# Four graph layers on one core: transformer blocks written out with norms by node tiles across the seams, graph convolution joined to them, and another order of VectorE's work in the one-hot sums

## The chip, the core and the metric

One Trainium2 chip, one of its cores. A core has TensorE (matrix products into PSUM), VectorE, ScalarE and GpSimd (elementwise work), SyncE (here only the start of DMAs) and 16 DMA engines. Each engine runs its own list of instructions in order and waits on semaphores for the others. The metric is the time of one execution on the device, in microseconds (us); the lower the better. In the profile TensorE's products are PE, its weight loads PEld, VectorE is DVE, ScalarE is ACT, GpSimd is POOL, SyncE is SP; a q behind a name means the engine's sequencer.

## What is computed

Four graph layers follow each other on 625 nodes with 512 features and 20,000 edges (src, dst), sorted by dst. Each gets h = relu(layernorm(x)) and adds its result to x:

```python
x = x + _L0(h)   # relu(mean of h[src] over the edges of dst @ W_l.T + b_l + h @ W_r.T)
x = x + _L1(h)   # four transformer blocks, below
x = x + _L2(h)   # graph convolution: sum of h[row]*norm over the edges, @ lin_w.T + lin_b
x = x + _L3(h)   # edge network with mish, sums by node, layernorm
...
for i in range(NUM_BLOCKS):                                   # 4
    y = _cond_layer_norm(x, cond, s1_w[i], s1_b[i], b1_w[i], b1_b[i])   # xn*(1+scale)+bias
    y = _sparse_attention(y, src, dst, wq[i], bq[i], wk[i], bk[i], wv[i], bv[i], wo[i], bo[i])
    x = x + y
    y = _cond_layer_norm(x, cond, s2_w[i], s2_b[i], b2_w[i], b2_b[i])
    y = jax.nn.relu(y @ m_w1[i] + m_b1[i]) @ m_w2[i] + m_b2[i]
    x = x + y
```

scale and bias come from a 16-wide vector per node (cond). Attention has 4 heads of 128 and runs over the edges; several equal edges count severally.

## The kernel before

The 625 nodes are padded to NP = 640, five node tiles of 128 rows (NT = 5); 512 features are four chunks (KF = 4). `build` runs four stages, each a block of its own with a barrier at its end: `front`, `transformer_layer`, `gcn_layer`, `edge_layer`.

**front** turns the edges into dense 640 x 640 matrices: how often an edge occurs, and its weight in two f16 parts. The edges go in 40 groups of 512. For a group VectorE compares the edges' targets with 64 node numbers (the to-comparison, L531) and the sources of three of its four tiles with all 640 (three from-comparisons, L535); ScalarE makes the fourth tile from |difference| (L334, L337); GpSimd multiplies the to-matrix by the weights (L314, 128x512 f16) as soon as the to-comparison is done; TensorE multiplies from and to (20 products of 192 columns into one of two PSUM places), and VectorE adds the result to `sums` (L556, PSUM and SBUF). `compare(u + 2, ...)` stands two groups ahead of the addition of group u. The loop is a hardware loop (`Fori`) with four groups per turn; two groups are compared ahead of it.

**transformer_layer** has a hardware loop over the four blocks. Every product with a weight matrix is made of f32r parts: high (rounded, by ScalarE, `high`) and low (the rest, by VectorE, `low`), and is three matmuls, hi*hi, hi*lo and lo*hi. A block on TensorE: norm(0) with v, then q and k (transposed, in parts of 384 and 256 nodes), attention in N = 20 steps of head and node tile (scores S, transposed probabilities T, and after each head's tiles the product o), wo by node tiles, norm(1), m1 (transposed), m2 by node tiles. Two PSUM banks `one` and three double banks `two` are handed out in a fixed order by `Plan`.

A norm, in the order of the engines: VectorE has the statistics of each tile (L1052) right behind the residual addition (L1050); after the fifth tile it aggregates all five (L1014), adds EPS (L1016); ScalarE takes the inverse root of all five by Ln and Exp (L178, L180); VectorE normalizes a tile (L1023) and scales it by TensorE's product of cond (L1029 after L840); TensorE turns it and adds the bias product (L832, L835); ScalarE takes the high part (L934) and VectorE the low part (L1036) out of PSUM. GpSimd adds the row bias to the residual r as soon as VectorE has normalized a tile (L791), and cuts the cond weights (L780). SyncE loads a weight matrix into one of two places when the matrix before in that place has been split.

**gcn_layer** loads the kept weight matrix (1600 KB) and lin_w, makes the norm on VectorE for all tiles, then eight sums of five products (`agg`) and five products with lin_w (`lin`). **edge_layer** is not changed.

## Time and profile before

| what | us |
|---|---|
| timed runs, median of 3 (lowest to highest) | 1864.12 (1862.62 to 1864.5) |
| the profiled execution, its own time | 1859.79 |
| its span, first to last instruction | 1858.1 |
| front (loop over the edge groups in it) | 0 to 212.4 (16.6 to 142.1) |
| transformer blocks | 212.4 to 966.4 |
| graph convolution | 966.4 to 1016.6 |
| edge network | 1016.6 to 1858.1 |
| busy: PE, DVE, ACT, POOL | 1640.7, 1258.9, 1028.6, 678.1 |

A row of the trace has the start of an instruction (or of several alike in a row), how long it or they took, the engine, the line, the operation, output and inputs by name with their sizes, and in brackets how long the engine had been idle before and what it had waited for. "issue" is idle time for which the profile shows no wait. The names C, tr_two and tr_one in the norm's rows are the normalized tile y, a `two` bank and a `one` bank.

### The profile page before, as it was taken

The page shows a single profiled execution, that of the slowest core. Times are in us where ns is not written, and L with a number is a line of the kernel's source. Part 1 is how long each engine was busy: PE and PEld are TensorE (multiplying, and loading weights), DVE is VectorE, ACT ScalarE, POOL GpSimd, SP SyncE. Part 2 cuts the span into 40 slices and gives each one's busy share as a digit, 9 for nine tenths or more (in the row PEclk, how much of TensorE's full clock was granted, in tenths as well). Part 3 has the DMA queues.
Part 4 walks back from the last instruction along what each step waited for, and adds up shares of the span by engine and source line. Part 5 has one row for each costly group of instructions (what it writes and reads, how often), then busy time and mean ns, then how long its engine had stood idle before and what let it go on. Part 6 is the DMA issues. An engine that isn't in the chain of part 4 may idle for free. (4 is left out here: it accounts for less than half of the span.)

```text
span 1858.1 us, 26597 instructions
## 1 busy us (share of the span) xinstructions
PE 1640.7 (88%) x8590; PEld 1278.8 (69%) x8590; DVE 1258.9 (68%) x1915; ACT 1028.6 (55%) x1292; POOL 678.1 (36%) x497
## 2 busy tenths in 40 slices
PE   4559699889988998899868879999999999999986
PEld 3555296679667966786654367777777777777863
DVE  8997646553646364536463358888888888888844
ACT  7643125232523262326131069999999999999822
POOL 2330100120012001200110277888888888888200
PEclk9999799989998999899889989999999999999988
DMA  2000421021102200220020676777777777778400
GB/s 94 0 0 1 147 60 46 1 69 58 45 1 70 80 23 6 70 74 23 6 86 30 207 161 144 143 140 149 145 141 147 145 141 148 146 139 186 91 29 29
DMA packets 109491, 158.94 MB, mean 86 GB/s; under 512 B 42459, under 2 KB 47579, under 8 KB 108803
## 3 DMA queue, kind: packets, MB, share of 16 engines
q0 software_dynamic: 74320, 89.02, 24.6%
q1 hardware_dynamic: 35090, 68.86, 11.7%
q8 instruction: 48, 0.79, 0.2%
q14 instruction: 33, 0.26, 0.0%
HBM read 145.73 MB, written 11.86 MB: 85 GB/s over the span
## 5 line engine op out<-in xcount | busy, mean ns | idle before, releaser
L1416 POOL DMA_INDIRECT edge_early<-dst_table,edge_index x160 | 311.3, 1946 | 63.9 <-issue 55.3
L194 PE MATMUL edge_z2p<-edge_w_hi,edge_h_hi 128*128 128x512 f32 x640 | 261.7, 409 | 0.4 <-issue 0.2
L791 POOL TENSOR_TENSOR tr_r<-tr_r,tr_row_b 128x512 f32<-128x512 f32 x40 | 54.8, 1393 | 565.2 <-DVE C L1023 565.2
L194 PE MATMUL edge_z2p<-edge_w_hi,edge_h_lo 128*128 128x512 f32 x640 | 253.6, 396 | 0.0
L194 PE MATMUL edge_z2p<-edge_w_lo,edge_h_hi 128*128 128x512 f32 x640 | 253.4, 396 | 0.0
L1385 POOL DMA_INDIRECT edge_early<-src_table,edge_index x160 | 175.1, 1094 | 96.5 <-issue 36.8
L194 PEld LDWEIGHTS edge_z2p<-edge_w_hi,edge_h_hi 128*128 128x128 f32 x640 | 120.5, 188 | 54.7 <-issue 29.1
L194 PEld LDWEIGHTS edge_z2p<-edge_w_hi,edge_h_lo 128*128 128x128 f32 x640 | 120.5, 188 | 29.2
L194 PEld LDWEIGHTS edge_z2p<-edge_w_lo,edge_h_hi 128*128 128x128 f32 x640 | 120.7, 189 | 25.3
L1684 DVE TENSOR_TENSOR edge_late<-edge_z2p,edge_b 128x1024 f32<-128x1024 f32 x80 | 97.9, 1224 | 51.3 <-PE edge_z2p L194 50.9
L194 PE MATMUL front_sum_ps<-front_to_onehot,front_from_onehot 128*128 128x192 f16 x800 | 74.7, 251 | 59.1 <-DVE front_sums L556 45.9
L959 ACT ACTIVATE tr_probs<-tr_scores,tr_nmax 128x640 f32<-128x640 f32 x80 | 66.2, 828 | 109.1 <-DVE tr_nmax L1080 106.2
L1080 DVE CUSTOM_DVE_ANT_0 tr_scores<-tr_two,logc 128x640 f32<-128x640 f32 x80 | 65.9, 824 | 85.7 <-PE tr_two L866 84.1
L194 PE MATMUL tr_one<-tr_yT_hi,tr_w_hi 128*128 128x256 f32 (+1 forms) x384 | 121.3, 316 | 2.6 <-DVE tr_kT L1068 2.6
L194 PE MATMUL tr_one<-tr_yT_lo,tr_w_hi 128*128 128x256 f32 (+1 forms) x384 | 119.9, 312 | 0.0
L194 PE MATMUL tr_one<-tr_yT_hi,tr_w_lo 128*128 128x256 f32 (+1 forms) x384 | 119.7, 312 | 0.0
L1701 DVE SCALAR_TENSOR_TENSOR edge_early<-edge_early,edge_z1p 128x1024 f32<-128x1024 f32 x80 | 97.3, 1217 | 31.7 <-ACT edge_early L1592 30.4
L194 PEld LDWEIGHTS front_sum_ps<-front_to_onehot,front_from_onehot 128*128 128x128 f16 x800 | 66.8, 100 | 67.1 <-issue 53.2
L1582 ACT ACTIVATE edge_early<-edge_z1p 128x1024 f32<-128x1024 f32 x80 | 80.5, 1006 | 50.3 <-PE edge_z1p L1471 50.3
L866 PE MATMUL tr_two<-tr_kT,tr_qT 128*128 128x320 f32 x320 | 100.9, 442 | 5.4 <-ACT tr_probsT L965 4.1
L1588 ACT ACTIVATE edge_early<-edge_early 128x1024 f32<-128x1024 f32 x80 | 84.4, 1055 | 36.7 <-DVE edge_early L1662 35.9
L1462 PE MATMUL edge_z1p<-ident,edge_early 128*128 128x128 f32 x640 | 84.8, 276 | 17.9 <-DMA edge_early<-dst_table,edge_index 13.2
(300 smaller groups left out, 4054.4 us busy)
## 6 DMA issues: line engine op xcount, KB each, us to landing
edge_attr<-in_attr_T SPq DMA_DIRECT2D x80, 128.0 KB
tr_w_raw<-in_m SPq DMA_DIRECT2D x8, 1024.0 KB, 5.3
tr_w_raw<-in_wv SPq DMA_DIRECT2D x5, 1024.0 KB, 5.3
tr_w_raw<-in_wq SPq DMA_DIRECT2D x5, 1024.0 KB, 5.4
agg<-edge_sum_rows POOLq DMA_DIRECT2D x37, 128.0 KB
tr_w_raw<-in_wk SPq DMA_DIRECT2D x4, 1024.0 KB, 7.4
tr_w_raw<-in_wo SPq DMA_DIRECT2D x4, 1024.0 KB, 5.3
tr_cw_raw<-in_cond_w SPq DMA_DIRECT2D x5, 768.0 KB, 5.6
```

Source lines behind the costliest of these rows:

```text
L194: mm = pe.matmul(out, a, b, start=(n == 0), stop=(n == last))
L791: pool.tensor_tensor(r[:, i, :], r[:, i, :], row_b[:, :], ALU.add).then_inc(bias_added, 1)
L866: mm = pe.matmul(bank[:, f, 0:HALF], qT[:, h, i * P:(i + 1) * P], kT[:, h, f * HALF:(f + 1) * HALF], start=True, stop=True)
L959: act.activation(probs[:, n % 3, :], scores[:, n % 2, :], ACT.Exp, bias=nmax[:, n:n + 1], scale=-1.0, accum_out=den[:, n:n + 1]).then_inc( ...
L1080: ins = dve.tensor_tensor_reduce(out=cols(scores[:, n % 2, :], HALF), in0=bank[:, :, 0:HALF], in1=cols(k.logc[:, i, :], HALF), scale=-1.0, ...
L1385: pool.indirect_dma_start(out=from_rows[a][:, j, :], out_offset=None, in_=k.src_table, in_offset=bass.IndirectOffsetOnAxis(ap=index[a // 2 ...
L1416: pool.indirect_dma_start(out=from_rows[ring][:, j, :], out_offset=None, in_=k.dst_table, in_offset=bass.IndirectOffsetOnAxis(ap=index[rin ...
L1462: mm = pe.matmul(z1[:, c, j * P:(j + 1) * P], from_rows[ring][:, j, c * P:(c + 1) * P], k.ident[:, :], is_transpose=True, start=(c % 2 == ...
L1582: act.activation(m1[one], ps_z1[one][:, :], ACT.Exp).then_inc(S["e1_ready"], 1)
L1588: act.activation(m1[one], m1[one], ACT.Square).then_inc(S["inner1_ready"], 1)
L1684: dve.tensor_tensor(cols(z2[two], D), cols(ps_z2[:, :], D), b2[:, None, :].to_broadcast([P, PT, D]), ALU.add).then_inc(S["z2_ready"], 1)
L1701: dve.scalar_tensor_tensor(m1[one], m1[one], 0.5, ps_z1[one][:, :], ALU.subtract, ALU.mult).then_inc(S["h1_ready"], 1)
```

## The change

Three things are changed.

1. In the one-hot loop `compare` is cut in two. VectorE's order in a group is now: to-comparison of group u + 2, addition of group u, three from-comparisons of group u + 2.
2. `transformer_layer` and `gcn_layer` become one function, `transformer_and_gcn`, and the loop over the blocks is a Python loop: the four blocks are written out in each engine's program, with constants where registers stood. A norm goes tile by tile and is laced into the products before it: behind the residual of a tile follow its statistics, their aggregate and the negated mean on VectorE, then on ScalarE Ln, Exp, mean times root and the normalized tile itself (an activation with bias and scale, in place of VectorE's L1023). TensorE has the scale product of tile i and the turning of tile i - 2 between two tiles of wo, or of m2 for the next block's norm; the last tile is turned within m1, or between the first two tiles of v. The scale product lies in the second half of a `two` bank, the turned tile in its first. For wo's first two tiles the products over the first three heads are made early, at steps 19 and 21 of attention. low("m1") and low("wv") go in four pieces, between steps or tiles. GpSimd adds the row bias after all five tiles are normalized; in the last block it also adds r to x.
3. The convolution lies behind the last block without a barrier. Its matrix is loaded when the last head's product has been read, its norm goes by tiles as above (with the factor `dis` on ScalarE), and its first two sums run over tiles 0 to 3 before tile 4 is added.

```diff
@@ front
-                        compare(u + 2, (a + 2) % RING, start_of(u + 2))
+                        compare_to(u + 2, (a + 2) % RING, start_of(u + 2))
                         start = start_of(u)
...
                             "p (i n w) -> p i n w", i=NT, n=4)[:, :, 0:3, :], ALU.add).then_inc(added, 1)
+                        compare_from(u + 2, (a + 2) % RING)
@@ TensorE
-                with pe.Fori(0, BLOCKS) as b:
-                    pe.wait_ge(block_done, b + 1)
-                    norm(0, b)
+                def step(b, s, i):
+                    scale(b, s, i)
+                    if i >= 2:
+                        feature_major(b, s, i - 2)
...
+                for b in range(BLOCKS):
+                    if b == 0:
+                        for i in range(NT):
+                            step(b, 0, i)
+                    feature_major(b, 0, 3)
+                    value(b, 0)
+                    feature_major(b, 0, 4)
+                    for i in range(1, NT):
+                        value(b, i)
...
+                        if n == N - 1:
+                            plan.open(pe, ("early", b))
+                            plan.need(pe, ("o", b, HEADS - 2, 1))
+                            wait_weights("wo", b)
+                            early(0)
+                        if n == N + 1:
+                            early(1)
...
                     for i in range(NT):
-                        by_node("wo", i, "wo", rows, b)
-                    norm(1, b)
+                        if i < 2:
+                            if i == 0:
+                                plan.need(pe, ("o", b, HEADS - 1, 0))
+                            plan.made(three(plan.at[("wo", b, i)].bank[:, :],
+                                            node_pairs(of_tile(rows, i), "wo", [HEADS - 1]), start=False))
+                        else:
+                            if i == 2:
+                                plan.need(pe, ("o", b, HEADS - 1, 1))
+                            by_node("wo", i, of_tile(rows, i), "wo", b)
+                        step(b, 1, i)
+                    feature_major(b, 1, 3)
...
                         for m in range(KF):
                             by_feature("m1", m, f, "m1", b)
+                            if (f, m) == (0, 1):
+                                feature_major(b, 1, 4)
...
-                        by_node("m2", i, "m2", (hid_hi, hid_lo, yT_hi, yT_lo), b)
+                        by_node("m2", i, hidden_tile(i), "m2", b)
+                        if b < LAST:
+                            step(b + 1, 0, i)
...
+                pe.wait_ge(loaded["gcn_W"], 16)
+                for m in range(2):
+                    plan.open(pe, ("agg", m, 0))
+                    neighbours(m, 0, range(NT - 1))
+                for m in range(2):
+                    plan.made(neighbours(m, 0, [NT - 1]))
@@ ScalarE
+                def inverse(i, factor=None):
+                    act.wait_ge(var_ready, inverse.n + 2)
+                    inverse.n += 1
+                    own(act.activation(k.rstd[:, i:i + 1], inverse.mv[:, i, 1:2], ACT.Ln, bias=eps[:, 0:1]))
+                    own.wait()
+                    own(act.activation(k.rstd[:, i:i + 1], k.rstd[:, i:i + 1], ACT.Exp, scale=-0.5))
+                    own.wait()
...
+                    own(act.activation(shift[:, i:i + 1], neg_mean[:, i:i + 1], ACT.Copy, scale=k.rstd[:, i:i + 1]))
+                    own.wait()
...
+                def step(b, s, i):
+                    if i >= 2:
+                        high_part(b, s, i - 2)
+                    inverse(i)
+                    act.activation(y[:, i, 0:D], r[:, i, :], ACT.Identity, bias=shift[:, i:i + 1],
+                                   scale=k.rstd[:, i:i + 1]).then_inc(y_ready, 1)
...
                     for i in range(NT):
+                        step(b, 1, i)
+                    high_part(b, 1, 3)
+                    plan.take(act, ("wo", b, NT - 1))
+                    high("m2", b)
+                    high_part(b, 1, 4)
@@ VectorE
+                def step(b, s, i):
+                    moments(i, r, st, mv)
+                    if i >= 2:
+                        low_part(b, s, i - 2)
+                    if i >= 1:
+                        scaled(b, s, i - 1)
...
+                    for i in range(NT):
+                        residual("wo", b, 0, i)
+                        step(b, 1, i)
+                    scaled(b, 1, NT - 1)
+                    low_part(b, 1, 3)
+                    low("m2", b)
+                    low_part(b, 1, 4)
...
+                    if b < LAST:
+                        for i in range(NT):
+                            residual("m2", b, 1, i)
+                            step(b + 1, 0, i)
+                            if i < PIECES:
+                                low_piece("wv", b + 1, i)
@@ GpSimd
-                            pool.wait_ge(read1, b * (2 * NT) + (s * NT + i + 1))
+                        pool.wait_ge(y_ready, of_norm(b, s, NT - 1))
+                        for i in range(NT):
                             pool.tensor_tensor(r[:, i, :], r[:, i, :], row_b[:, :], ALU.add).then_inc(bias_added, 1)
+                        if b < LAST:
+                            pool.wait_ge(bias_added, of_norm(b, s, NT - 1))
+                            cut(b + 1, s)
```

How the lists of two engines read before and now. First VectorE in the one-hot loop, one group; ISA and REGISTER_ALU rows are its sequencer's. Before:

```order
L525 TENSOR_LOAD starts
L525 ISA x2
L531 ISA
L531 TENSOR_TENSOR front_to_onehot<-front_iota,front_dst 128x4x64
L535 ISA
L535 TENSOR_SCALAR front_from_onehot<-front_iota,front_src_f 128x640
...
L552 REGISTER_ALU
L556 ISA
L556 TENSOR_TENSOR front_sums<-front_sums,front_sum_ps 128x15x64
```

and now:

```order
L556 TENSOR_TENSOR front_to_onehot<-front_iota,front_dst 128x4x64
L550 TENSOR_LOAD starts
L550 ISA x2
L582 REGISTER_ALU
L586 ISA
L586 TENSOR_TENSOR front_sums<-front_sums,front_sum_ps 128x15x64
L564 ISA
L564 TENSOR_SCALAR front_from_onehot<-front_iota,front_src_f 128x640
```

The addition to front_sums has moved from behind the three from-comparisons to between them and the to-comparison.

VectorE again, at the seam from wo to m1, from the fourth wo tile before:

```order
L1050 TENSOR_TENSOR tr_r<-tr_r,tr_one 128x512
L110 REGISTER_ALU
L1052 BN_STATS tr_st<-tr_r 128x6
L76 REGISTER_ALU
L1014 BN_AGGR tr_mv<-tr_st 128x2 x5
L76 REGISTER_ALU
L1016 TENSOR_SCALAR rstd<-tr_mv 128x5
L1017 REGISTER_ALU
L1023 TENSOR_SCALAR C<-tr_r,tr_mv,rstd 128x512 x2
```

and now, third and fourth tile:

```order
L1222 TENSOR_TENSOR tr_r<-tr_r,tr_one 128x512
L1193 BN_STATS tr_st<-tr_r 128x6
L1195 BN_AGGR tr_mv<-tr_st 128x2
L1197 TENSOR_SCALAR tr_neg_mean<-tr_mv 128x1
L1209 TENSOR_TENSOR tr_yT_lo<-tr_two,tr_yT_hi 128x4x128
L1202 SCALAR_TENSOR_TENSOR C<-tr_two,C 128x512
L1222 TENSOR_TENSOR tr_r<-tr_r,tr_one 128x512
```

Each tile now has its own aggregate, and the low part of the tile two before and the scaling of the tile before stand ahead of the next residual.

TensorE at the same seam, before: the last products of wo, then the norm.

```order
L194 MATMUL tr_one<-tr_w_hi,tr_yT_lo 128x512
L825 REGISTER_ALU
L110 REGISTER_ALU
L840 MATMUL tr_one<-tr_cw,condT 128x512
L110 REGISTER_ALU
L840 MATMUL tr_one<-tr_cw,condT 128x512
L110 REGISTER_ALU x2
L832 MATMUL tr_two<-ident,C 128x128 x4
L835 MATMUL tr_two<-condT,tr_cw 128x128 x4
```

Now, at the end of wo's third tile and the start of its fourth:

```order
L883 MATMUL tr_one<-tr_w_lo,tr_yT_hi 128x512
L883 MATMUL tr_one<-tr_w_hi,tr_yT_lo 128x512
L911 MATMUL tr_two<-tr_cw,condT 128x512
L919 MATMUL tr_two<-ident,C 128x128 x4
L922 MATMUL tr_two<-condT,tr_cw 128x128 x4
L883 MATMUL tr_one<-tr_w_hi,tr_yT_hi 128x512
```

The scale product and the turning of an earlier tile stand between two tiles of wo. TensorE's program has 2934 such rows, before 1452.

## Rows read from the trace of the kernel before

**Rows 1.** Busy us (count) by stretch: PE, PEld, DVE, ACT, POOL; clock; DMA.

```profile
16.64:142.09 125.45, 74.74 (x800) 66.76 (x800) 125.42 (x209) 69.00 (x107) 47.59 (x40) 1.00 0.00 2
391.84:575.00 183.16, 164.27 (x816) 133.34 (x815) 95.47 (x177) 64.78 (x114) 18.51 (x12) 0.93 0.14 44
```

**Rows 2.** The same view, one group of the loop, and the last but one.

```profile
103.61:106.68 3.07, 1.81 (x20) 1.61 (x20) 3.07 (x6) 1.54 (x3) 1.19 (x1) 1.00 0.00 0
137.39:139.68 2.29, 1.81 (x20) 1.61 (x20) 2.29 (x6) 0.00 (x0) 0.00 (x0) 1.00 0.03 7
```

**Rows 3.** Timeline (start, us, engine, line, operation): the same two groups.

```profile
103.61 0.41 DVE L531 TENSOR_TENSOR front_to_onehot<-front_iota,front_dst 128x256 f16 x1
...
104.53 1.16 DVE L535 TENSOR_SCALAR front_from_onehot<-front_iota,front_src_f 128x640 f16<-128x640 f16 x1
...
104.32 1.19 POOL L314 TENSOR_TENSOR front_to_onehot<-front_to_onehot,front_wb 128x512 f16<-128x512 f16 x1 [1.88 <-DVE front_to_onehot L531]
105.61 1.14 DVE L556 TENSOR_TENSOR front_sums<-front_sums,front_sum_ps 128x960 f32 x1
...
137.73 0.97 DVE L535 TENSOR_SCALAR front_from_onehot<-front_iota,front_src_f 128x640 f16<-128x640 f16 x3
```

**Rows 4.** Busy by stretch as in rows 1: seams, attention, the last m2.

```profile
362.00:376.27 14.27, 10.57 (x47) 9.33 (x45) 11.40 (x22) 2.81 (x6) 6.85 (x5) 0.63 0.08 20
...
406.60:420.43 13.83, 7.67 (x29) 6.51 (x30) 9.41 (x19) 1.90 (x5) 6.85 (x5) 0.62 0.14 52
...
465.00:511.00 46.00, 42.02 (x200) 29.21 (x199) 28.33 (x70) 26.38 (x51) 0.00 (x0) 1.00 0.13 45
...
943.98:958.70 14.72, 14.16 (x62) 11.00 (x60) 9.94 (x11) 4.53 (x5) 4.79 (x2) 1.00 0.00 0
958.70:972.90 14.20, 0.02 (x1) 0.00 (x0) 12.32 (x28) 1.70 (x3) 0.00 (x0) 0.65 0.38 135
```

**Rows 5.** Timeline of PE: the last head, the norm, in m1.

```profile
341.28 5.64 PE L194 MATMUL tr_one<-C,tr_v 128*128 128x320 f32 x20 [0.87 <-ACT C L965]
...
366.59 1.12 PE L832 MATMUL tr_two<-ident,C 128*128 128x128 f32 x4 [3.14 <-DVE C L1029]
...
379.25 0.36 PE L194 MATMUL tr_one<-tr_yT_hi,tr_w_hi 128*128 128x384 f32 x1
```

**Rows 6.** Waits of PE (us in total, times, longest): loop's turn; all blocks.

```profile
PE tr_one L840 <- issue: 4.2, 1, 4.2
...
PE tr_two L874 <- DVE tr_probs L1090: 17.7, 40, 1.3
```

**Rows 7.** Timeline: the convolution's first product, and the last sum's copy.

```profile
973.40 0.87 PE L194 MATMUL gcn_p<-gcn_W,gcn_h 128*128 128x320 f32 x1 [14.68 <-DMA gcn_W<-W_kept]
...
996.81 0.44 ACT L1148 ACTIVATE gcn_aggT<-gcn_p 128x320 f32<-128x320 f32 x1 [2.25 <-PE gcn_p L194]
```

**Rows 8.** Timeline of the norm between wo and m1.

```profile
362.20 0.69 DVE L1050 TENSOR_TENSOR tr_r<-tr_r,tr_one 128x512 f32<-128x512 f32 x1 [1.33 <-PE tr_one L194]
362.92 0.69 DVE L1052 BATCH_NORM_STATS2 tr_st<-tr_r 128x6 f32<-128x512 f32 x1
...
364.45 0.21 ACT L178 ACTIVATE rstd<-rstd 128x5 f32<-128x5 f32 x1 [17.05 <-DVE rstd L1016]
...
365.55 1.50 POOL L791 TENSOR_TENSOR tr_r<-tr_r,tr_row_b 128x512 f32<-128x512 f32 x1 [129.94 <-DVE C L1023]
365.85 0.68 DVE L1029 SCALAR_TENSOR_TENSOR C<-tr_one,C 128x512 f32<-128x512 f32 x1
```

**Rows 9.** Timeline: an activation with bias and scale in front.

```profile
52.12 0.80 ACT L365 ACTIVATE front_h<-x,front_shift,rstd 128x512 f32<-128x512 f32 x1
```

**Rows 10.** Timeline of PE: a tile turned among v, q's start in blocks 2 and 1.

```profile
424.70 0.60 PE L832 MATMUL tr_two<-ident,C 128*128 128x128 f32 x4
...
437.62 0.34 PE L194 MATMUL tr_one<-tr_yT_hi,tr_w_hi 128*128 128x384 f32 x1
...
253.18 0.34 PE L194 MATMUL tr_one<-tr_yT_hi,tr_w_hi 128*128 128x384 f32 x1
```

674 lines of the change are left out of this document (359 added, 315 removed).

## Prediction

> **What bounds the kernel now.** I read the sums by stretch first [rows 1]. Up to 142 us VectorE is busy all the time (the one-hot loop), from 212 to 1017 us TensorE is the fullest engine but has holes, and the edge stage, 841 us, is not touched by the change. So two things are to be found: what fills VectorE in the loop, and what makes TensorE's holes at the seams of a transformer block.
>
> In the loop one group of edges takes 3.07 us on VectorE, the last groups only 2.29 us [rows 2]. The difference is one instruction: of three equal comparisons the third lasts 1.16 us and ends at 105.69, 0.18 us after GpSimd's multiplication ended at 105.51 [rows 3]. The last two groups have no multiplication left. So the multiplication holds the comparison. TensorE (1.81 of 3.07 us) and ScalarE (1.54) wait for VectorE, not it for them [rows 2].
>
> In a block, read the clock and TensorE's busy time in the seams [rows 4]. Between the end of the wo products and the start of m1 14.3 us pass, between m2 and v 13.8 us, at 0.62 and 0.63 of the full clock; the clock sinks to its lower level (1.2 GHz) after the idle 3.14 us [rows 5] and comes back only inside m1. What TensorE waits for is the norm: all five tiles' statistics, then one root, then the tiles. Between two blocks comes 4.2 us in which TensorE waits for nothing shown ("issue"), at the turn of the loop [rows 6]. Before the graph convolution a barrier, a load and a norm leave TensorE idle for 14.68 us [rows 7].
>
> **1. The loop's order.** Nothing is added or removed. A group's order was to-comparison, three from-comparisons, addition; it becomes to-comparison, addition, three from-comparisons. From [rows 3], counted from the start of the to-comparison: the next VectorE instruction starts at 0.33, GpSimd starts at 0.71 (104.32 less 103.61) and ends at 1.90. The addition (1.07 from start to start) now lies under it, and the first from-comparison starts at 1.40. It is held to 1.90 and ends 0.18 later, 2.08, in place of 1.40 + 0.37 = 1.77 (0.37 is a comparison unheld: 0.97 for three, overlapped). So 0.31 us of holding stays, the group takes 2.29 + 0.31 = 2.60, and 0.47 us fall away in each of the 38 groups with a multiplication: **18 us**. Bounds: no holding left, 38 x 0.78 = 30; nothing gained, 0. Next late would be TensorE: its group starts after the comparisons, takes 1.81 and is wanted 0.33 us after the start of the group after next: 1.1 us of slack. ScalarE has 1.0.
> This rests on the addition (one operand in PSUM) not being held itself. The row for it: the scaling at 365.85, also with one operand in PSUM, takes 0.68 us beside a GpSimd addition that runs from 365.55 to 367.05 [rows 8]. Were it otherwise, GpSimd would start at 1.47, end at 2.66, the comparison at 2.84, and the group would take 3.36, 11 us more in all.
> The Trainium skill, SBUF — State Buffer, section "SBUF: two separate sides", says that VectorE and GpSimd take a shared port in turn, whole instruction by whole instruction, and that VectorE needs it in its two-port modes or with two SBUF inputs. By that rule the addition is free, as forecast (18 us); with the port taken by every VectorE instruction it would be the 11 us more.
>
> **2. The wo-m1 seam, four times.** The norm now runs tile by tile between the products. Per tile, with spacings from [rows 8]: VectorE 0.72 (residual) + 0.72 (statistics) + 0.20 + 0.17 (two small ones, by ScalarE's 0.21) = 1.81, then 0.62 each for scaling and low part, 3.05 in all. ScalarE: four small ones of 0.24 (L178 is 0.21) = 0.96, a new 128x512 activation with bias and scale, 0.80 [rows 9], and the high part 0.60: 2.36. TensorE: 2.75 for twelve products (m2: five times as many end 14.7 us after 943.98, 0.5 of it a wait and 0.4 the last one's length [rows 4]), 0.25 scale, 0.85 for turning (424.70 to 425.55) [rows 10]: 3.85. No engine is full, but tile i's chain (1.81, 1.76, 0.7, 0.85, 0.6, 0.62) is 6.3 us long and VectorE keeps strict order. Going down the three lists from the end of the last head's product: wo tiles 2, 3, 4 start at 1.9, 6.3 and 10.1, the turning of tile 2 ends at 14.0, that of tile 3 waits for VectorE until 16.2 (a hole of 2.2), m1 starts at 17.1. Tile 4 is turned inside m1 (0.85); ScalarE, in order, reads the first m1 bank only after it, and the two banks of the ring make m1 wait another 1.8. m2 starts at 33.8. Before it took 341.28 + 5.64 to 391.84 = 44.9 [rows 1, 5].
> Against that, 18 products of wo now run early, in attention, two pieces of 2.06 us. The first needs the low part of head 2, which VectorE makes after the probabilities of step 18, some 2.1 us after TensorE is free, and both stand ahead of what the last head needs: its product starts 3.7 us later (4.1 of work and 2.1 of waiting, less the idle time that was there: 1.3 and 0.3 for probabilities [rows 6], 0.9 before the product [rows 5]). So 44.9 - 33.8 - 3.7 = 7.4 a block, **30 us**. GpSimd's bias additions now start after the fifth tile and fall beside low("m2"), which is wanted only 14 us later; that cover hides them. Bounds: 3 to 11 a block.
>
> **3. The m2-v seam, three times.** The same chain between m2's five tiles, with four pieces of low("wv") on VectorE (0.66 each, an estimate by size: 128x512, like the residual's 0.69), and without the loop's turn. Down the lists: m2 tiles at 0, 3.0, 6.0, 9.9, 13.7, v at 20.6, q at 35.2. Before: 391.84 to 437.62 = 45.8 [rows 1, 10]. **10.6 each, 32 us**; 4.2 of it is the turn. GpSimd stands in this order behind a cut that waits for ScalarE's, so its bias additions fall beside low("wq"), which one of them can hold for its 1.5 us [rows 8]: q has 1.3 to spare, cost 0.2. Bounds: 6 to 14.
>
> **4. The graph convolution joined.** Its matrix and weights are loaded during the last seam, the norm goes by tiles, and GpSimd has added x and r before m2 is done. The first two sums run over tiles 0 to 3 (8 x 0.54 = 4.3 us), longer than tile 4's chain of 1.81 + 1.2 + 0.8 = 3.8. Before: m2's start 943.98 to the last sum's end 996.8 = 52.8 [rows 4, 7]. Now 13.8 for m2, 0.2, and 8 x 2.70 = 21.6: 35.6. **17 us**; bounds 12 and 19.
>
> **5. Small terms.** low("m1") in four pieces: TensorE waited 17.7 us in all for probabilities [rows 6]; I take a quarter of it as due to the whole one on VectorE and gone with the pieces, **4 us**, bounds 0 and 8. In the first block there was no turn of a loop, and ScalarE, free only after its two cuts and high("wv"), now makes the tiles one at a time, with low("wv") between them on VectorE: v starts at 239.7, q at 256.8, before 253.18 [rows 10]: **-4 us**; bounds -7 and 0.
>
> Sum: 18 + 30 + 32 + 17 + 4 - 4 = **97 us**. The profiled execution took 1859.8, which gives 1763; the median of the three timed runs is 4.3 higher, 1864.1, and the forecast is made there: **1767 us**.
>
> **The rivals.**
> A, the clock: at each wo-m1 seam a hole of 2.2 us stays, and idle 3.14 us were followed by 12.7 us at 1.2 GHz (366.6 to 379.3) [rows 5]. If the holes of 2.2 do the same, m1 runs at half clock for as long and loses 6.3 us a block: 25 us, 1792. For it: nothing in the trace shows what 2.2 us do. Against: attention has a hole at nearly every step, up to 1.3 us, and its stretch stands at 1.00 [rows 4]. The Trainium skill, TensorE: Matmul & The Clock Gate, section "A second HAM failure mode: psum-queue depth-cycling", says that small idle times between groups of products make the clock swing; by it A holds and more (attention too), and the attention row speaks against it.
> B, the loop gains nothing: the comparison behind the addition is held as long as before, because GpSimd starts later than I count. 1785; with the addition itself held, 1796. Against it are the two rows named in 1.
> C, slower than before: written out, the blocks are no loop any more, and TensorE's program is 2934 rows in place of 1452, each run once. If code arrives late, as at the loop's turn (4.2 us), each such halt costs 4.2 us; from 23 halts, six a block, the whole gain is gone, and at eight a block it is 134 us, 1901. For: the halts at the turn exist. Against: the front and the first and last 16 steps of the edge stage are written out too, and their rows show no such halt.
> D, the change doesn't do what it says: order inside VectorE makes the tile chains serial, a seam saves only the loop's turn and part of the clock: 3 us a seam in place of 7.4 and 10.6, 1767 + 40 = 1807.
>
> **How the numbers follow.** Forecast 0.66, with terms that move together about 1750 to 1784; A 0.15; B 0.09; D 0.07; C 0.03. Two in ten may be left out: the range is 1745 to 1796. Upwards it takes in A and B, downwards the loop free of holding (up to 12 us more) and the seams' upper bounds in part. About 0.2% (4 us) is what a measurement can tell from no change. All cases but C lie beyond it below: faster 0.96, same 0.01, slower 0.03.
>
> **What would show it.** The loop's group at 2.6 us, the first comparison (not the third) long. No "issue" of 3 to 4 us between blocks. From m2 to m2 of the next block about 183.2 - 7.4 - 10.6 - 1 = 164 us [rows 1]. TensorE's clock in the seams at 1.00 (A: lower). TensorE's wait before the first sum of the convolution under 1 us. It is wrong if comparisons are held elsewhere, if the early wo pieces delay the last head by much more than 3.7, or if TensorE shows many new waits for "issue".

## The result

Over four runs of each the kernel after takes 1769.95 us (median; 1763.32 to 1773.72) and the kernel before 1864.31 us: a ratio of 0.9488, 95% interval 0.9457 to 0.952. The forecast was 1767, the range 1745 to 1796. The profiled execution of after took 1770.9 us, its span is 1769.2 us; that is 88.9 us less than the span of before.

The page of after, its line of busy times. VectorE's busy time falls by 52 us, 24 of it in the loop, where comparisons were held; ScalarE's rises by 65, above all because it now makes the norm's tiles.

```profile
PE 1615.3 (91%) x8590; PEld 1259.4 (71%) x8590; DVE 1206.8 (68%) x1912; ACT 1093.3 (62%) x1476; POOL 684.2 (39%) x500
```

The sums by stretch of after (columns as in [rows 1]): two lines from the one-hot loop, one group each; four wo-m1 seams, from the start of the last head's product to the start of m2; three m2-v seams, from the start of m2 to the start of q; and the graph convolution, from the start of m2 to the end of the last sum.

```profile
95.21:97.66 2.45, 1.82 (x20) 1.60 (x20) 2.45 (x7) 1.58 (x3) 1.04 (x1) 1.00 0.00 0
97.66:100.11 2.45, 1.82 (x20) 1.60 (x20) 2.45 (x7) 1.54 (x3) 1.04 (x1) 1.00 0.00 0
...
322.69:365.18 42.49, 38.37 (x205) 33.96 (x203) 22.49 (x40) 20.22 (x42) 8.32 (x5) 0.92 0.10 32
494.59:535.52 40.93, 36.80 (x205) 32.38 (x204) 23.11 (x40) 20.23 (x42) 8.35 (x5) 0.96 0.10 33
664.51:703.87 39.36, 35.24 (x204) 30.81 (x203) 23.10 (x40) 20.23 (x42) 8.35 (x5) 1.00 0.10 34
831.23:873.68 42.45, 38.34 (x204) 33.95 (x203) 24.55 (x40) 20.22 (x42) 15.46 (x10) 0.92 0.11 39
365.18:402.21 37.03, 34.93 (x168) 29.12 (x166) 23.69 (x41) 16.69 (x33) 7.30 (x4) 0.95 0.11 26
535.52:572.55 37.03, 34.92 (x167) 29.00 (x166) 23.61 (x41) 16.69 (x33) 7.29 (x4) 0.95 0.10 26
703.87:739.31 35.44, 33.33 (x167) 27.77 (x166) 23.71 (x41) 16.69 (x33) 7.29 (x4) 1.00 0.09 31
...
873.68:909.11 35.43, 35.43 (x143) 26.50 (x142) 12.27 (x27) 13.41 (x34) 0.00 (x0) 1.00 0.00 0
```

The loop's group takes 2.45 us, before 3.07 [rows 2]. The convolution takes 35.43 us, before 52.8. The seams are the part to look at: the same work takes 42.5, 40.9, 39.4 and 42.5 us, and the granted clock is 0.92, 0.96, 1.00 and 0.92; 37.0, 37.0 and 35.4 us at 0.95, 0.95 and 1.00. At full clock a wo-m1 seam takes 39.4 us and an m2-v seam 35.4 us, and the others are longer by 1.6 us or twice that; 1.6 us is what one fall to the lower clock costs here. Over the seven seams it is 3.1 + 1.6 + 0 + 3.1 + 1.6 + 1.6 + 0 = 11.0 us.

The timeline of TensorE in the first block of after shows the holes (in brackets the idle time before the row): ahead of the first early piece of wo, ahead of the turning of the fourth tile, and inside m1.

```profile
317.36 0.47 PE L883 MATMUL tr_two<-tr_w_hi,tr_yT_hi 128*128 128x512 f32 x1 [2.10 <-ACT C L1145]
...
344.42 1.12 PE L919 MATMUL tr_two<-ident,C 128*128 128x128 f32 x4 [2.11 <-DVE C L1202]
...
353.70 0.44 PE L883 MATMUL tr_one<-tr_yT_hi,tr_w_hi 128*128 128x384 f32 x1 [1.63 <-ACT tr_qT L1165]
```

By stretch, with the times of both profiled executions:

| Stretch | before | after | forecast | measured |
|---|---|---|---|---|
| up to q of block 1 (loop, first norm) | 253.2 | 231.6 | 18 - 4 = 14 | 21.6 |
| q to m2, four blocks | 555.4 | 532.6 | 30 + 4 = 34 | 22.9 |
| m2 to q of the next block, three times | 135.4 | 109.5 | 32 | 25.9 |
| last m2 and convolution sums | 52.8 | 35.4 | 17 | 17.4 |
| behind them | 861.3 | 860.1 | 0 | 1.2 |
| sum | 1858.1 | 1769.2 | 97 | 88.9 |

From m2 to m2 of the next block 170.3, 168.4 and 169.8 us pass, where the prediction named 164 as a sign.

### The profile page after: what moved, and what is told of

The parts are those of the page before. It is cut to its first block and busy times, and to the rows that moved or that the text cites. A ratio compares the mean times of both kernels' runs of the same rounds, so it can differ in the third digit from the quotient of the medians.

```text
span 1769.2 us, 25359 instructions
## 1 busy us (share of the span) xinstructions
PE 1615.3 (91%) x8590; PEld 1259.4 (71%) x8590; DVE 1206.8 (68%) x1912; ACT 1093.3 (62%) x1476; POOL 684.2 (39%) x500
## 5 line engine op out<-in xcount | busy, mean ns | idle before, releaser
L867 POOL TENSOR_TENSOR tr_r<-tr_r,tr_row_b 128x512 f32<-128x512 f32 x40 | 64.7, 1650 | 289.4 <-ACT C L1099 289.1
L856 POOL TENSOR_TENSOR tr_cw<-tr_cw_raw,tr_cw 32x1024 fp32r<-32x1024 f32 x8 | 19.4, 2425 | 374.4 <-ACT tr_cw L1063 374.3
```

## The experiments

Each was timed against the kernel before on one chip, in four to ten executions; e2_small_mult has one. The median of before moved between 1858 and 1865 us from one group of runs to the next, so ratios are compared. The theory: three effects carry the change (the port held in the loop; a chain by tiles in place of a barrier at each seam; the barrier before the convolution), and what is missing at the seams is the clock, which falls behind holes of about 2 us. The rivals: the sizes of single pieces (the early products of wo, the split of m1's matrix) were wrong, or the blocks written out cost something of their own.

### The loop's order alone (e1_loop_alone)

Edit on the kernel before:

```
-                        compare(u + 2, (a + 2) % RING, start_of(u + 2))
+                        compare_to(u + 2, (a + 2) % RING, start_of(u + 2))
...
                         dve.tensor_tensor(into, into, ps[a % 2][:, 0:NT * 4 * WIN].rearrange(
                             "p (i n w) -> p i n w", i=NT, n=4)[:, :, 0:3, :], ALU.add).then_inc(added, 1)
+                        compare_from(u + 2, (a + 2) % RING)
```

> The kernel before with one edit, the order inside the one-hot loop (to-comparison, addition, three from-comparisons). Theory: the loop's gain is independent of everything later, so the group takes 2.44 us as in the trace of after, 38 x 0.63 = 24 us go, about 1840 us, ratio 0.987. Rival (the prediction's own size): GpSimd's multiplication keeps its 1.19 us, group 2.60, 18 us, 1846, ratio 0.990. Second rival: part of the early start of the blocks came from something else than the loop, then the loop alone gives less than 18.

Measured: 1838.12 us against 1864.93, ratio 0.9881 (0.9851 to 0.9912). In its trace a group takes 2.44 us. So the loop gives 16 to 28 us by itself, which leaves room for 18 as well as 24; the group decides, by it 38 x 0.63 = 24. The first theory holds. Why 2.45 and not 2.60 shows in the timeline of after:

```profile
95.21 0.41 DVE L556 TENSOR_TENSOR front_to_onehot<-front_iota,front_dst 128x256 f16 x1
95.55 1.14 DVE L586 TENSOR_TENSOR front_sums<-front_sums,front_sum_ps 128x960 f32 x1
95.92 1.04 POOL L339 TENSOR_TENSOR front_to_onehot<-front_to_onehot,front_wb 128x512 f16<-128x512 f16 x1 [1.41 <-DVE front_to_onehot L556]
96.61 0.53 DVE L564 TENSOR_SCALAR front_from_onehot<-front_iota,front_src_f 128x640 f16<-128x640 f16 x1
```

GpSimd's multiplication starts 0.71 us after the to-comparison, as forecast, and ends at 96.96. The first from-comparison starts at 96.61, lasts 0.53 us in place of 0.37 and ends 0.18 us after the multiplication. Everything is as the prediction put it but the length of the multiplication: 1.04 us, not 1.19 [rows 3]. Before, it ran beside comparisons; now it runs beside an addition from PSUM. In after itself both lengths stand: the multiplications of the first two groups, which still have comparisons beside them, take 1.13 and 1.18 us, all later ones 1.04. So comparisons lengthen it, and the addition doesn't. That is 0.15 us a group, 38 times: the missing 5.7 us.

### A smaller multiplication, old order (e2_small_mult)

Edit on the kernel before (one of four tiles is multiplied; the other three are set to zero once, so their weighted sums are left out):

```
-  pool.tensor_tensor(to_onehot[a][:, :, 1:3, :], to_onehot[a][:, :, 0:1, :].to_broadcast(shape),
-                     weights[:, :, :, None].to_broadcast(shape), ALU.mult).then_inc(weighted, 1)
+  small = [P, 1, 2, WIN]
+  pool.tensor_tensor(to_onehot[a][:, 0:1, 1:3, :], to_onehot[a][:, 0:1, 0:1, :].to_broadcast(small),
+                     weights[:, 0:1, :, None].to_broadcast(small), ALU.mult).then_inc(weighted, 1)
```

> The kernel before, old order of the loop, but GpSimd multiplies only one of the group's four tiles (the sums of the other three are left out, so the output is not the reference's). Theory (the multiplication holds the third comparison until its own end): with a multiplication that ends before the third comparison starts, the three comparisons take 0.97 us together, the group 2.29 to 2.35 us in place of 3.07, about 28 us in all. Rival (the third comparison is slow because of its place before an addition that reads PSUM, or because of ScalarE's two activations): group stays at 3.0 us or above.

Measured, one execution: 1833.87 us. The timeline, one group:

```profile
103.47 1.11 DVE L539 TENSOR_SCALAR front_from_onehot<-front_iota,front_src_f 128x640 f16<-128x640 f16 x3
103.84 0.56 POOL L318 TENSOR_TENSOR front_to_onehot<-front_to_onehot,front_wb 128x128 f16<-128x128 f16 x1 [1.88 <-DVE front_to_onehot L535]
```

The group takes 2.43 us (103.13 to 105.56). The multiplication ends at 104.40, and the third comparison ends 0.18 us later, at 104.58; the three take 1.11 us, where 0.97 is free of holding. So the group is not at the 2.29 to 2.35 us that were expected: the short multiplication, too, ends after the third comparison has begun, and holds it for what is left. By the group it is 24 us, by the single time 31. The order is the old one, ScalarE does what it did: only the multiplication is shorter. So it holds the comparison, as the prediction had it; the rivals (place, ScalarE) fall. The Trainium skill, SBUF — State Buffer, section "SBUF: two separate sides", says that VectorE and GpSimd take the shared port whole instructions at a time, VectorE only in its two-port modes or with two SBUF inputs. These traces agree: 1.16 us beside 0.37 for the comparison, and 1.14 us for the addition with one operand in PSUM, before and after, alone or beside the multiplication.

### The blocks written out, nothing else (e3_written_out)

Edit on the kernel before, on all five engines:

```
-                with pe.Fori(0, BLOCKS) as b:
+                for b in range(BLOCKS):
```

> The kernel before with the four blocks written out on all five engines in place of a loop; nothing else is changed. Theory: what goes is VectorE's 3.0 us of waiting for nothing shown at each of three turns, on the path there: 9 us (the prediction took 4.2 a turn from TensorE's wait, 12.6), 1852 to 1855, ratio 0.993 to 0.995. Rival C: code that is run once arrives late: new waits of 3 to 4 us for nothing shown inside the blocks, no gain or a loss. Third: the turn is hidden by the norm that follows, ratio 1.000.

Measured: 1851.34 us against 1864.93, ratio 0.994 (0.9923 to 0.9958). VectorE's timeline at the first turn, of before and then of this kernel:

```profile
411.05 0.45 DVE L1014 BATCH_NORM_AGGREGATE tr_mv<-tr_st 128x2 f32<-128x6 f32 x5 [3.01 <-issue]
```

```profile
410.14 0.45 DVE L1014 BATCH_NORM_AGGREGATE tr_mv<-tr_st 128x2 f32<-128x6 f32 x5
```

VectorE's wait for nothing shown is 3.01, 2.57 and 2.48 us at the three turns, 8.1 together, and is gone in all three. The three m2-v seams take 126.8 us in place of 135.4: 8.6. Seam by seam it is 4.9, 1.1 and 2.5 us, for the lower clock lasts a different time in each; only the sum fits the waits. The prediction had taken TensorE's wait of 4.2 us, its longest (all three have 10.2); VectorE's stood on the path, since the norm begins there. No new wait for "issue" appears on TensorE inside the blocks: rival C falls.

### No early pieces of wo (e6_no_early)

Edit on the kernel after: the first two tiles of wo are computed whole behind the last head.

```
-                        if n == N - 1:
-                            plan.open(pe, ("early", b))
-                            plan.need(pe, ("o", b, HEADS - 2, 1))
-                            wait_weights("wo", b)
-                            early(0)
-                        if n == N + 1:
-                            early(1)
```

> The kernel after without the early pieces of wo: the first two node tiles of wo are computed whole after the last head. Theory by the prediction's numbers: the last head starts 3.7 us sooner in each block, the seam has 4.1 us more of products: 0.4 a block slower, so 1.6 us, ratio to before 0.950 against 0.949. Rival: the early pieces delay the last head by less than they save or the wait of 2.1 us ahead of the first one is not made up for: 0 to 3 us a block either way.

Measured: 1782.22 us, ratio 0.9566 (0.9535 to 0.9597). After is at 0.9488 and, in the second measurement below, at 0.952: the pieces are worth 9 to 14 us, and not the 1.6 that were expected. In the two profiled executions it is 13.2 us. From the end of k to the last head's product the time falls by 2.5, 3.0, 3.0 and 4.1 us (3.7 were taken), 12.7 in all; the 4.1 has a fall of the clock in after, so without it the delay is 2.5 to 3.0. From there to m2 it rises by 24.4: four times the 4.1 us of products, and the head's product itself runs slower, 8.3 us in all:

```profile
321.70:329.50 7.80, 7.80 (x21) 5.28 (x22) 0.49 (x1) 0.44 (x1) 0.00 (x0) 0.72 0.00 0
493.40:500.70 7.30, 7.29 (x21) 5.01 (x22) 0.49 (x1) 0.44 (x1) 0.00 (x0) 0.77 0.00 0
667.40:674.70 7.30, 7.30 (x21) 5.01 (x22) 0.49 (x1) 0.44 (x1) 0.00 (x0) 0.77 0.00 0
840.10:848.20 8.10, 8.05 (x21) 5.44 (x22) 0.49 (x1) 0.44 (x2) 0.00 (x0) 0.70 0.03 10
```

In after the head takes 5.54 us in all four blocks, here 7.3 to 8.1 at clock 0.70 to 0.77. The early pieces fill the end of attention, where TensorE otherwise waits 1.35, 0.78 and 0.79 us in a row for the last steps, and keep the clock. In the kernel before it is the same: its last heads take 5.6, 7.3, 5.7 and 7.2 us. Of the 13.2 us the blocks hold 24.4 - 12.7 = 11.7; another 2 stand ahead of q of the first block, where the edit changes nothing.

### After again (after_again)

> The kernel after, unchanged, as the measure for the three others. Theory (what is left of the seams' loss is the clock, which falls in some seams and not in others): the seams' times differ between this execution and the one shown (wo-m1 seam from the last head's start to m2 39.4, 40.9 or 42.5 us; m2-v seam 35.4 or 37.0), each time with the granted clock; at clock 1.00 they are 39.4 and 35.4. Rival: the same seams are slow in every execution, with a cause of their own. Ratio 0.946 to 0.952.

Measured: 1768.67 us (1763.09 to 1780.33), ratio 0.952 (0.947 to 0.957). Its seams:

```profile
494.40:533.90 39.50, 35.37 (x205) 30.99 (x204) 23.16 (x40) 20.25 (x42) 8.35 (x5) 1.00 0.10 34
828.50:870.90 42.40, 38.27 (x205) 33.86 (x204) 23.98 (x40) 20.24 (x42) 15.43 (x10) 0.92 0.11 39
365.00:402.00 37.00, 34.89 (x167) 28.98 (x166) 23.73 (x41) 16.71 (x33) 7.26 (x4) 0.95 0.11 27
533.90:569.40 35.50, 33.39 (x168) 27.77 (x167) 23.56 (x41) 16.71 (x33) 7.33 (x4) 1.00 0.10 27
```

Again 39.4 and 35.4 us at clock 1.00 and the same steps above it, but in other blocks: the second block's seams took 40.9 and 37.0 us in the first execution and take 39.5 and 35.5 here. The work is the same; what differs is whether the clock falls. The holes behind which it may fall are there in every block. The other runs fit: over the eight executions of after the shortest (1763.1 and 1763.3 us) have the highest mean clock, 0.977, and the longest (1780.3) the lowest, 0.968.

### The hole filled (e4_fill8)

Edit on the kernel after:

```
+                    if i == 3:
+                        for _ in range(8):
+                            pe.matmul(bank[:, :], k.condT[:, i * P:(i + 1) * P], cw[:, 2 * s, :], start=True, stop=True)
                     plan.need(pe, ("scale", b, s, i))
```

> The kernel after, with eight more products of the scale kind (their result is overwritten) ahead of the turning of the fourth tile in every norm, where TensorE waits 2.1 us. No work is saved. Theory (the hole of 2.1 us is what makes the clock fall): the granted clock behind it stays at 1.00 and the seams go to 39.4 and 35.4 us, up to 11 us less, 5 us at least as the holes of 1.6 and 1.5 behind ScalarE stay: ratio 0.943 to 0.946. Rival (the clock falls by chance, or through the number of products before, not the hole): the same ratio as after, 0.949, or slower by the extra products.

Measured: 1765.41 us, ratio 0.9491 (0.9461 to 0.9522). The expected time was missed: at least 5 us less were named, and the ratio is the rival's. The time alone decides nothing. The stretches behind the hole do, first of after and then of this kernel (the same place, the first block, some 2 us later in this execution), then this kernel's seams:

```profile
342.00:344.00 2.00, 0.30 (x3) 0.16 (x2) 1.90 (x6) 1.33 (x4) 0.00 (x0) 1.00 0.00 0
344.00:346.00 2.00, 1.58 (x8) 1.59 (x9) 1.05 (x2) 0.87 (x2) 0.93 (x1) 0.57 0.04 8
346.00:348.00 2.00, 2.00 (x9) 2.00 (x9) 0.69 (x1) 1.69 (x2) 2.00 (x3) 0.58 0.00 0
348.00:350.00 2.00, 2.00 (x13) 2.00 (x12) 1.18 (x1) 0.72 (x1) 2.00 (x2) 1.00 0.00 0
```

```profile
344.00:346.00 2.00, 2.00 (x12) 1.56 (x10) 1.90 (x6) 1.29 (x4) 0.00 (x0) 1.00 0.00 0
346.00:348.00 2.00, 1.78 (x14) 1.54 (x13) 1.09 (x2) 1.37 (x3) 0.88 (x1) 1.00 0.00 0
348.00:350.00 2.00, 2.00 (x13) 2.00 (x12) 0.69 (x1) 1.96 (x2) 2.00 (x3) 1.00 0.00 0
524.00:528.00 4.00, 4.00 (x16) 4.00 (x15) 1.41 (x3) 1.05 (x2) 0.00 (x0) 0.59 0.68 121
...
324.70:364.10 39.40, 37.17 (x213) 32.17 (x212) 23.13 (x40) 20.26 (x42) 8.34 (x5) 1.00 0.10 34
493.20:534.20 41.00, 38.77 (x213) 33.81 (x213) 23.12 (x40) 20.25 (x42) 8.34 (x5) 0.96 0.12 32
663.10:702.50 39.40, 37.18 (x212) 32.22 (x211) 23.13 (x40) 20.25 (x42) 8.35 (x5) 1.00 0.11 34
829.80:869.30 39.50, 37.27 (x212) 32.30 (x212) 25.32 (x40) 20.25 (x42) 16.05 (x10) 1.00 0.12 43
364.10:399.50 35.40, 35.19 (x175) 29.10 (x174) 23.70 (x41) 16.72 (x33) 7.27 (x4) 1.00 0.11 28
534.20:569.60 35.40, 35.19 (x175) 29.07 (x174) 23.60 (x41) 16.72 (x33) 7.28 (x4) 1.00 0.11 28
702.50:738.00 35.50, 35.28 (x176) 29.16 (x175) 23.67 (x41) 16.72 (x33) 7.30 (x4) 1.00 0.09 30
```

Behind the hole of 2.11 us after stands at 0.57 and 0.58; with the hole filled, at 1.00. Six of seven seams are at 1.00, where the two executions of after have two and four of seven. The one at 0.96 falls inside m1 (0.59 from 524 to 528 us), behind ScalarE's hole of 1.6 us, which was not filled. Is it more than chance? Behind this hole, where it is not filled, the clock fell at 4, 2, 3, 2 and 6 of seven places in the traces of after, after_again, e10, e9 and e6, at 17 of 35 in all; filled, at none of seven. So work without use, put into the hole, keeps the clock up behind it; this rests on one execution with seven places. The seams take 265.6 us together, where those of after take 274.7 and 270.1. The gain in the median, 3 to 5 us, is within the scatter: two falls behind the hole of 2.10 us at the end of attention stay (486.3 and 824.2 us), and q of the third block waits 2.38 us here, 1.23 in after.

### Another order at the seams (e5_order)

Edit on the kernel after, TensorE's part (the other engines follow; ScalarE makes m2's high part in four pieces between the first tiles of m1, and wk's between two of q):

```
-                    feature_major(b, 0, 3)
                     value(b, 0)
+                    feature_major(b, 0, 3)
+                    value(b, 1)
                     feature_major(b, 0, 4)
...
-                    feature_major(b, 1, 3)
...
-                            if (f, m) == (0, 1):
-                                feature_major(b, 1, 4)
+                            if f == 0 and m < 2:
+                                feature_major(b, 1, 3 + m)
```

> The kernel after with another order on the same work: the first product group of v stands ahead of the turning of the fourth tile, the first of m1 too; ScalarE makes the high part of m2's matrix in pieces between the first four tiles of m1 and that of wk after two of q. Theory: TensorE's holes go from 2.11 + 1.63 to about 1.4 us in the wo-m1 seam (2.3 x 4), from 2.1 + 1.4 to nearly none in the m2-v seam (3.5 x 3) and 2 us in the first block, and about 8 us come from the clock: 30 us less than after, about 1740, ratio 0.933. Rival: the pieces make ScalarE or VectorE late inside m1 (1.8 us of ScalarE for 2.1 of TensorE), m2 starts later, and half of it is lost: 0.941.

Measured: 1752.25 us, ratio 0.9432 (0.94 to 0.9465): the gain of the rival, but not by its mechanism. The wo-m1 seams take 37.0 to 38.7 us and the m2-v seams 33.2. What was lost lies in three places. At full clock an m2-v seam gains 2.2 us, and 3.5 were named. Three of the four wo-m1 seams still have a fall of the clock (0.59 from 504.7 to 508.5 us), behind a new wait of 1.56 us at the start of m1. And in q of the second and third block TensorE waits 2.06 and 3.43 us for ScalarE, with the clock at 0.68 from 565 to 570 us, around the longer one.

### The first early piece later (e7_order_early)

```
-                        if n == N - 1:
+                        if n == N:
                             plan.open(pe, ("early", b))
```

> As e5_order, and the first early piece of wo stands behind the transposes of step 18 and no longer ahead of them. Theory: the transposes (0.7 us) go into the wait of 2.10 us ahead of the early piece, and the last head starts 0.4 to 0.7 us sooner in each block: 2 to 3 us less than e5_order, ratio 0.932. Rival: the transposes start late themselves, and the wait only moves: no change.

Measured: 1743.66 us, ratio 0.9369 (0.934 to 0.9399), 0.0063 less than e5_order: 8.6 us, where 2 to 3 were expected. From the end of k to the last head 61.1 to 61.6 us pass in place of 61.9 to 63.3, and three of the four wo-m1 seams take 37.0 us, where one did. The moved transposes are 0.5 us a block of this, 2.2 in all, as expected; the rest goes with the clock, whose mean over a run is 0.975 to 0.980 here and 0.968 to 0.973 in e5_order. The hole in q is still there. ScalarE's and SyncE's timeline show its cause:

```profile
391.92 0.44 SPq L799 DMA_DIRECT2D tr_w_raw<-in_wk  x1
...
399.75 1.91 ACT L1072 ACTIVATE tr_w_hi<-tr_w_raw 128x2048 fp32r<-128x2048 f32 x1 [3.06 <-DMA tr_w_raw<-in_wk]
```

ScalarE waits for the load of wk, which SyncE issued at 391.92 us. Its buffer was free some 17 us sooner (the next kernel shows it); ahead of it in SyncE's queue stood the load of the next conditioning weights, which waited for GpSimd's cut (387.05 to 391.52).

### The load first (e8_load_first)

Edit on the kernel just above (e7_order_early); besides, ScalarE makes wk's high part at its old place:

```
-                    if b < LAST:
-                        sp.wait_ge(cw_ready, b * 2 + 2)
-                        load_cw(b + 1)
                     sp.wait_ge(w_split, of_weight("wv", b) + PIECES)
                     load("wk", b)
+                    if b < LAST:
+                        sp.wait_ge(cw_ready, b * 2 + 2)
+                        load_cw(b + 1)
```

> As e7_order_early, but ScalarE makes wk's high part at its old place (behind the last tile of v), and SyncE issues the load of wk ahead of that of the next conditioning weights, whose wait (GpSimd's cut of this block's, which stands behind ScalarE's work on wq) came first. Theory: the hole of 3.3 us (ScalarE waits for wk's load, TensorE for ScalarE) inside q in the second and third block, new in e5 and e7, was the load issued 9 us after its buffer was free; it goes, with the low clock behind it, and from q to the last head all blocks take about 90 us in place of 94 and 96: 10 us less than e7_order_early, about 1734, ratio 0.932. Rival: wk's load now takes bandwidth from wq's, q starts later by as much: same as e7, 0.937.

Measured: 1735.79 us (1733.85 to 1736.64), ratio 0.9319 (0.9298 to 0.9341): the time that was expected. The load is issued at 374.68 us, and all seven seams stand at full clock (four of them here):

```profile
374.68 0.37 SPq L799 DMA_DIRECT2D tr_w_raw<-in_wk  x1
...
321.10:358.10 37.00, 35.06 (x204) 30.78 (x204) 22.73 (x43) 20.37 (x45) 7.43 (x5) 1.00 0.06 18
801.60:838.50 36.90, 34.96 (x204) 30.73 (x203) 25.58 (x41) 20.38 (x45) 14.60 (x10) 1.00 0.13 45
358.10:391.30 33.20, 33.20 (x167) 27.74 (x167) 22.60 (x41) 16.70 (x33) 4.51 (x2) 1.00 0.14 53
678.60:711.80 33.20, 33.20 (x167) 27.71 (x166) 22.57 (x41) 16.70 (x33) 4.55 (x2) 1.00 0.16 54
```

From q to q of the next block it is 160.3, 160.3 and 160.2 us, and the five runs lie within 2.8 us, where those of after spread over 10 and 17; their mean clock is 0.978 to 0.980. This kernel is faster than both: 34 us below after. The sum: 2.4 x 4 and 2.2 x 3 us in the seams at full clock, 2.7 of the hole in q, 12.3 of the clock (11.0 in the seams, 1.3 in the fourth block's attention), 0.6 x 4 at the end of attention: 33.6.

### Two single pieces (e9_m1_whole, e10_load_only)

The split of m1's matrix whole, as before, in the kernel after:

```
-                        if n == 4:
+                        if n == 2:
                             plan.take(act, ("k", b, KF - 1, 1))
...
-                        if 4 <= n < 4 + PIECES:
-                            act.activation(w_hi[0][:, n - 4, :], w_raw[0][:, n - 4, :], ACT.Copy).then_inc(w_high, 1)
+                            high("m1", b)
...
+                        if n == 3:
+                            low("m1", b)
...
-                        if 5 <= n < 5 + PIECES:
-                            low_piece("m1", b, n - 5)
```

> The kernel after, with the high and low part of m1's matrix made whole at steps 2 and 3 of attention, as in the kernel before, in place of four pieces at steps 4 to 8. Theory by the prediction: the pieces take a quarter of TensorE's waits for probabilities away, 4 us in all; without them 4 us slower, ratio 0.951. Rival: the whole one falls where nothing waits for long, 0 to 1 us; or it makes one long wait at which the clock falls, then 5 us or more.

Measured: 1782.36 us, ratio 0.9574 (0.9546 to 0.9603), against 0.9488 and 0.952 of after: 10 to 16 us slower. The waits of TensorE for probabilities, in total, times and the longest, of after and then of this kernel:

```profile
PE tr_two L974 <- DVE tr_probs L1290: 10.0, 32, 0.8
```

```profile
PE tr_two L974 <- DVE tr_probs L1290: 16.3, 40, 1.2
```

These are 6.3 us, and 3.9 us are new waits for the transposed probabilities. From the end of k to the first head's product 18.5 us pass in place of 16.4, in each block. So the pieces are worth 8 us, twice the 4 that were taken. The rest of the time lies in q (its hole is 2.3 us here) and in falls of the clock.

The load of wk first, alone, in the kernel after:

> The kernel after, with one edit: the load of wk is issued ahead of the load of the next conditioning weights. Theory: TensorE's wait of 1.2 to 1.5 us inside q (second and third block, 2.7 in all) is ScalarE's wait for this load and goes: 3 us less than after, ratio 0.947. Rival: ScalarE's 1.9 us for wk's high part stands ahead of the reading of q's banks and makes the hole by itself: no change.

Measured: 1769.58 us (1765.16 to 1776.26), ratio 0.9503 (0.9469 to 0.9537): no change that can be told. The wait in q is gone from TensorE's waits all the same (q and k take 28.6 to 29.1 us in every block, in after up to 30.3); three of its four wo-m1 seams and all its m2-v seams had a fall of the clock, one of them twice as long (38.4 us for the seam, clock 0.91). A gain of 3 us can't be seen in the median of a kernel whose clock falls by chance.

## Why the prediction was right, and where it was not

**The loop's order: mechanism right, size low.** 18 us were forecast, 24 came by the group. The term that was mis-sized is the multiplication's length, 1.19 us taken from a row in which it was held itself; it measured 1.04. That the first comparison would be the long one, and end 0.18 us after the multiplication, came as written.

**The seams by tiles: right at full clock.** Going down the lists gave 33.8 us from the end of the last head to m2, with the head 39.4, and 35.2 for the m2-v seam. Measured at clock 1.00: 39.4 and 35.4. The hole ahead of the fourth tile was put at 2.2 and measures 2.11, the wait in m1 at 1.8 and measures 1.63.

**The step that failed is the clock.** "TensorE's clock in the seams at 1.00" is wrong in five of seven seams. Rival A had the mechanism: holes of 2.2 us let the clock fall. It was priced by the long hole of before, 6.3 us a fall in each wo-m1 seam and nothing elsewhere, 25 us. Shown is: a fall costs 1.6 us (seldom twice that), there may be two in a wo-m1 seam (behind the hole of 2.11, and inside m1 behind that of 1.63) and one in an m2-v seam, and it comes or not from one execution to the next. In sum 11.0 us in the first execution.

The row held against A was read wrongly. The stretch of attention at 1.00 (465 to 511 us) has single holes up to 1.1 us; the hole of 1.3 lies behind it, and right there, in the same trace, the clock falls:

```profile
523.45 0.76 PE L874 MATMUL tr_two<-ident,tr_probs 128*128 128x128 f32 x5 [1.26 <-DVE tr_probs L1090]
524.53 0.77 PE L874 MATMUL tr_two<-ident,tr_probs 128*128 128x128 f32 x5 [0.32 <-DVE tr_probs L1090]
```

```profile
526.16:533.44 7.28, 7.28 (x20) 4.65 (x20) 0.49 (x1) 0.44 (x1) 0.00 (x0) 0.77 0.00 0
```

Behind the holes of 1.26, 0.32 and 0.87 us the last head runs at 0.77, in this and in the fourth block; in the first and third it runs at 1.00. So the trace of before already had short holes followed by a short fall in two blocks of four, which speaks for rival A at a lower price. The Trainium skill, TensorE: Matmul & The Clock Gate, section "A second HAM failure mode: psum-queue depth-cycling", has small idle times between groups of products make the clock swing; the seams agree (0.92 to 1.00 with holes of 2.1 and 1.6 us), and so does the end of attention before, while the middle of attention, with holes up to 1.1 us at 1.00, does not.

**The sum of the two middle lines.** q to m2 fell short by 11 us. The seams lack 7.6 of them, and the clock alone is 7.8. Attention lacks the other 3.1: the hole in q in the second and third block (1.46 and 1.23 us), which was seen nowhere in the prediction, and the clock in the fourth (0.98). Of the 6 us that the m2-v seams lack 3.2 are the clock and 2.0 come from taking block 1 for typical: before, that seam took 45.8, 44.3 and 45.3 us.

**The early pieces and the split of m1.** The delay was put at 3.7 us and is 2.5 to 3.0, 4.1 with a fall of the clock in it; but the pieces are worth more than 0.4 us a block, as they hold the clock up at the end of attention. The split's pieces were worth 8 us, not 4. Against that stands a piece of the change that the prediction left out: ScalarE and GpSimd now cut the next block's conditioning weights inside attention, and the scaling of a probability tile beside GpSimd's cut lasts 1.49 us in place of 0.61:

```profile
287.50 2.58 POOL L856 TENSOR_TENSOR tr_cw<-tr_cw_raw,tr_cw 32x1024 fp32r<-32x1024 f32 x1 [66.58 <-ACT tr_cw L1063]
...
288.94 1.49 DVE L1290 TENSOR_SCALAR tr_probs<-tr_probs,tr_den,has 128x640 f32<-128x640 f32 x1
```

That head's stretch takes 15.6 us, before 14.95. Between the other heads some tenths are longer too; why was not tried.

**The convolution and the turn.** 17 forecast, 17.4 measured, TensorE busy for the whole 35.43 us. The joined convolution was not tried by itself; that it is worth this is read from the two traces. The turn of the loop was worth 8.6 us in three seams, beside 8.1 us of VectorE's waits; three times 4.2 had been taken.

**Why the total was near.** The loop and the first norm gave 7.6 us more than forecast, the stretch behind 1.2 more, the blocks 17 less. 97 against 88.9 in the profiled pair; in the medians 94.4, because the profiled execution of before lies 4.5 us under its median. So the parts were further off than the total, and their errors cancel: that much is luck.

**Rivals.** A came in part, at less than half its price. B and D fell by the trace (2.45 us a group; the chain by tiles at its forecast length), C by the kernel with nothing but the blocks written out, which is 11 to 14 us faster.

## What to carry to other kernels

When the barrier of a norm is replaced by a chain of tiles, go down the engines' lists by hand: at full clock the seams' lengths and their holes came out within 0.2 us. Then ask of each hole that is left what stands behind it in the same list and needs nothing of it; product groups and matrix splits moved into holes, and one load moved ahead of another's wait, gave 34 us more here, because the holes cost their length and the clock behind them. Where a kernel's runs scatter by 10 us and the shortest have the highest mean clock, look for holes of some 2 us on TensorE: with those of 2.1 us gone the scatter went down to 3, though four of 1.56 stayed.

## What the runs showed of the hardware

Not expected: the same hole in the same kernel is followed by the lower clock in some executions and blocks and not in others. In the two executions of after it was so behind 6 of 14 holes of 2.11 us in the seams, behind 3 of 8 of 2.10 us at the end of attention, and behind 4 of 8 of 1.63 us inside m1. Filled with useless products, the hole of 2.11 was not followed by a fall at any of seven places. The cost in these two executions was 1.6 us each time (the two stretches of 2 us at 0.57 and 0.58 are one such fall) but for one of 3.1, where the clock stayed low twice as long.

Length alone does not decide. A wait of 1.56 us at the start of m1 was followed by a fall in three blocks of four in e5_order, in one in e7_order_early and in none in e8_load_first. A single hole of 1.35 us at the end of attention was in none of eight (e7 and e8), while 1.35, 0.78 and 0.79 us in a row were in four of four (e6). What tells them apart is open, and so it is not shown that the last kernel's clock stays up in every execution; its five runs, at 0.978 to 0.980, speak for it.

An instruction that is slow beside another may be held itself in the row that its length is taken from: GpSimd's multiplication took 1.19 us against comparisons and 1.04 against an addition from PSUM.
